# Input weights in quarters, GpSimd adding a token's two weighted expert rows, and later expert weight preparation, in a cross-attention and mixture-of-experts kernel

## The chip, the cores and the metric

The kernel runs on one core of one Trainium2 chip. The metric is device time in microseconds (us) of one execution. Before the change it is 1564.54 us, the median of 3 runs (1563.1 to 1567.49).

## What is computed

```python
x = x + xattn(layernorm(x), ctx_768, Wq, Wkv, Wproj, bproj)   # 16 heads of 64, softmax over 128 keys
x = x + ffn(layernorm(x), gate_w, expert_w, expert_b, combine_w)

# ffn, for each token:
probs = softmax(tokens @ gate_w.T)                 # 8 experts
w, idx = top_k(probs, 2)
expert_out = silu(tokens @ expert_w[e].T + expert_b[e])
mixed = w[0] * expert_out[idx[0]] + w[1] * expert_out[idx[1]]
out = mixed @ combine_w.T
```

There are 64 sequences of 128 tokens with 256 features, and a context of 128 rows of 192 features for each. All is float32. Products are made of three matrix products on operands split into a rounded high part and a rest (names ending in `_hi` and `_lo`).

## The kernel before, in words

Two sequences make a pair; there are 32 pairs, numbered i. A pair has 8 slots, one for each pair of heads, numbered u = 0 to 7; the slot number s is 8i + u. Every engine runs its own instruction stream over the same slots, in an order written out by hand, and semaphores tie the streams together. In slot s TensorE turns the probabilities of the slot before (`turn_probs`, tile pT_ps), makes queries and keys three slots ahead (`queries_keys`, qk_ps), scores one slot ahead (`scores`, s_ps), then "mid" jobs, then `attend` (o_ps) and `project` (proj_ps) for earlier slots, then "late" jobs. Slots -8 to -1 are the lead-in, and slots from 256 on are the tail.

Per slot ScalarE makes exponentials and high parts, VectorE row maxima, row sums and low parts. GpSimd normalises the probabilities (L1392), splits the attended rows (L1401 and L1403, `o_s_hi` and `o_s_lo`, which `project` waits for), issues indirect DMAs (scatters L1424, gathers L1437) and, where u = 0, adds the bias (L1410). Project for slot s needs the `o_s_lo` that GpSimd makes in the same slot.

The last four pairs (28 to 31) take all experts densely in the tail. The first 28 go through a sorted copy of their rows: blocks of 128 rows of one expert (`turn_block`, `expert`, in slots 78 to 259), and then a mix for each pair. For the mix of pair m GpSimd gathers four row sets of 128x256 into `got` (a part of `stage`), ScalarE multiplies them by their weights (`weigh`, L935) in a slot t of `plan.mix`, TensorE turns and adds them (`turn_mixed`, L681) in the mid of slot t + 1, VectorE makes the low part `mT_s_lo`, TensorE multiplies by the combine weights (`combine`) late in slot t + 2, and VectorE adds the residual (L1092) in slot t + 3. 23 mixes have t + 1 in a slot up to 256: eleven of them fall on u = 0 and eleven on u = 2 (in couples: 128 and 130, 136 and 138, 144 and 146, and so on), and one on slot 256. The gather of pair m waits until `turn_mixed` of pair m - 2 has read the same buffer.

The mid and late jobs share three PSUM banks, `gen_ps`, in turn: a job waits until the third job before it in the order has been drained.

The weights come in through `stage`. The first loads bring two of the eight head pairs' query and key columns (FIRST) and all values (VALUES); the other six follow as REST. ScalarE rounds them (L835), VectorE and GpSimd make the low parts: `weight_lo` on VectorE (L1012 for queries, L1016 for the rest) and on GpSimd (L1374). GpSimd has the REST keys and the projection (L1415, L1374). The `queries_keys` of head pair 2 waits for all of REST. Expert weights are loaded into `stage` from slot -1 on, prepared in slots 1 to 9 (VectorE L1027, ScalarE L835, GpSimd L1374) and stored to an expert table.

Of the kernel before, what the change touches and what calls it, by code (L numbers as in the profile page):

```python
# [5 lines left out]
P = 128  # L6
# [52 lines left out]
class Plan:  # L59


    def __init__(self, pairs):
# [42 lines left out]
        self.tail = [r for at, r in sorted(self.mix.items()) if at > SLOTS * pairs + 2]  # L105
        self.last = max(max(self.turn) + 4, max(self.mix) + 4)
        self.jobs_at, order = {}, []
        for s in range(-SLOTS, self.last + 1):
# [45 lines left out]
def xattn_moe_kernel(nc, x, ctxT, wq, wkv, wkv_rest, wproj, bproj, gateT, expertT, expert_b, combineT, out):  # L154
# [20 lines left out]
    with ExitStack() as stack:  # L175
# [55 lines left out]
        def carve(n, rows):  # L231
# [83 lines left out]
        w_in = [sem(f"w_in{n}") for n in range(12)]  # L315
# [39 lines left out]
        ctx_lo, probs_done, weighted = (  # L355
            sem(n) for n in ("ctx_lo", "probs_done", "weighted"))
# [17 lines left out]
        def blocks_in_ring(r, n):  # L374
# [4 lines left out]
        FIRST, REST, VALUES = slice(0, 2 * P), slice(2 * P, D), slice(D, 2 * D)  # L379
        raw_wq = stage[:, 0, :].rearrange("p (a n) -> p a n", a=2)  # L380
        in_wq = wq.rearrange("(a p) n -> p a n", p=P)
        WEIGHTS = [
            (in_wq[:, :, FIRST], raw_wq[:, :, FIRST]),
            (wkv[0:P, FIRST], stage[:, 1, FIRST]),
            (wkv_rest[:, FIRST], stage[:, 2, FIRST]),
            (wkv[0:P, VALUES], stage[:, 1, VALUES]),
            (wkv_rest[:, VALUES], stage[:, 2, VALUES]),
            (in_wq[:, :, REST], raw_wq[:, :, REST]),
            (wkv[0:P, REST], stage[:, 1, REST]),
            (wkv_rest[:, REST], stage[:, 2, REST]),  # L390
# [7 lines left out]
        SPLIT = [  # L398
            (raw_wq[:, :, FIRST], *[w[:, :, FIRST] for w in wq_s]),
            (stage[:, 1, FIRST], *[w[:, FIRST] for w in wkv0_s]),  # L400
            (stage[:, 2, FIRST], *[w[:, FIRST] for w in wkvr_s]),
            (stage[:, 1, VALUES], *[w[:, VALUES] for w in wkv0_s]),
            (stage[:, 2, VALUES], *[w[:, VALUES] for w in wkvr_s]),
            (raw_wq[:, :, REST], *[w[:, :, REST] for w in wq_s]),
            (stage[:, 1, REST], *[w[:, REST] for w in wkv0_s]),
            (stage[:, 2, REST], *[w[:, REST] for w in wkvr_s]),
            (stage[:, 3, :], *[w[:, :, :].rearrange("p g n -> p (g n)") for w in wproj_s]),
        ]
# [3 lines left out]

        FOR_FIRST, FOR_VALUES, BY_VECTOR, PROJECTION, EXPERTS_FROM, COMBINE_SPLIT = 3, 5, 6, 8, 9, len(SPLIT) - 1
        KEYS_BY_POOL = PROJECTION - BY_VECTOR
        PROJ_BY_POOL = KEYS_BY_POOL + 1
# [3 lines left out]
        def _(sp):  # L419
# [29 lines left out]
            def load_weights(n):  # L449

                if n >= EXPERTS_FROM:
                    sp.wait_ge(w_lo_dve, BY_VECTOR)
                if n > EXPERTS_FROM:
                    sp.wait_ge(w_lo_pool, KEYS_BY_POOL)
                of, to = WEIGHTS[n]
                sp.dma_start(to, of).then_inc(w_in[n], 16)
# [66 lines left out]
            for s, i, u in slots():  # L523
# [16 lines left out]
                if s == -1:  # L540
                    load_weights(EXPERTS_FROM)
                if s == 0:
# [6 lines left out]
                if s == 1:  # L549
                    load_weights(EXPERTS_FROM + 2)  # L550
                if 2 <= s < E - RING + 2:
                    load_last(s - 2 + RING)
                if 2 <= s < E + 2:
                    keep_expert(s - 2)
                if i == 1 and u == 0:
# [15 lines left out]
                if s - 3 in plan.mix:  # L571
                    r = plan.mix[s - 3]
# [3 lines left out]
                if s - 1 in plan.mix:  # L576
                    r = plan.mix[s - 1]
# [10 lines left out]
        def _(pe):  # L588
# [9 lines left out]
            def queries_keys(j, p):  # L598
# [4 lines left out]
                if j == 0 and p == 0:  # L603
                    pe.wait_ge(w_hi, FOR_FIRST)
                    pe.wait_ge(w_lo_dve, FOR_FIRST)
# [147 lines left out]
            def general(s, position):  # L753
                for kind, n in plan.jobs_at[s, position]:
# [32 lines left out]
            pe.wait_ge(const_b, 2)  # L787
            for s, i, u in slots():
# [29 lines left out]
        def _(act):  # L818
# [6 lines left out]
            def weight_hi(n):  # L825
# [9 lines left out]
                act.activation(hi, raw, ACT.Copy, scale=QSCALE if n in (0, FOR_VALUES) else 1.0).then_inc(w_hi, 1)  # L835
# [95 lines left out]
            def weigh(m):  # L931
                act.wait_ge(gathered[m % 2], 64 * (m // 2 + 1))
                act.wait_ge(top_w_done, m + 1)
                for k in range(4):
                    last = act.activation(got[m % 2][:, k, :], got[m % 2][:, k, :], ACT.Copy, scale=top_w[:, m, k:k + 1])  # L935
# [13 lines left out]
            for s, i, u in slots():  # L949
# [38 lines left out]
                if i == -1 and u == 5:  # L988
                    for n in range(FOR_VALUES, PROJECTION):
                        weight_hi(n)  # L990
                if 2 <= s < E + 2:
                    weight_hi(EXPERTS_FROM + s - 2)
# [3 lines left out]
                if i == 1 and u == 2:  # L996
# [4 lines left out]
        def _(dve):  # L1001
# [6 lines left out]
            def weight_lo(n):  # L1008
                dve.wait_ge(w_hi, n + 1)
                raw, hi, lo = SPLIT[n]  # L1010
                if n in (0, FOR_VALUES):
                    dve.scalar_tensor_tensor(out=lo, in0=raw, scalar=QSCALE, in1=hi.bitcast(F32),  # L1012
                                             op0=ALU.mult, op1=ALU.subtract).then_inc(w_lo_dve, 1)
                else:
                    rows = HALF if n in (2, 4) else P
# [518 lines left out]
```

## Time and profile before

| what | value |
|---|---|
| median of 3 runs | 1564.54 us |
| the profiled execution's own time | 1565.96 us |
| its span in the trace | 1564.2 us |
| TensorE matmul busy | 1499.4 us, 96% of the span |
| VectorE busy | 1279.3 us, 82% |
| ScalarE busy | 1071.5 us, 69% |
| GpSimd busy | 942.5 us, 60% |

PE is TensorE (PEld its weight loads), DVE VectorE, ACT ScalarE, POOL GpSimd, SP the engine that issues most DMAs. Times are from the start of the span. In rows, a bracket at the end gives the idle time of the engine before the instruction and what ended it. TensorE's rows overlap: an instruction's duration is longer than the step to the next, so steps between starts are what it costs on the path.

### The profile page before, as it was taken

To read this page: it belongs to the slowest core of one execution; us is meant where nothing else is said; L and a number is where in the kernel's file an instruction comes from. 1 tells how busy PE (TensorE), PEld (TensorE's weight loads), DVE (VectorE), ACT (ScalarE), POOL (GpSimd) and SP (SyncE) were. 2 spreads that over 40 slices of the span, in tenths; PEclk is the share of its full clock that TensorE was granted. 3 is DMA by queue.
4 is the path that set the end of the run, shared out by engine and by line. 5 is a ranking of instruction groups with operands and counts; after the bars stand their busy time and mean duration, and the time that the engine had idled before them with its cause. 6 is when DMAs were issued, how large, how long until landed. Compare 5 with 4: busy or idle time off the path is not lost.

```text
span 1564.2 us, 38447 instructions
## 1 busy us (share of the span) xinstructions
PE 1499.4 (96%) x11664; PEld 1435.4 (92%) x11664; DVE 1279.3 (82%) x3121; ACT 1071.5 (69%) x2923; POOL 942.5 (60%) x1239
## 2 busy tenths in 40 slices
PE   5999999999999999999999999999999999999878
PEld 5889999999899999999899999989999999999767
DVE  6978888888988888888988888888888888877556
ACT  4767666666677766777677676767776767667645
POOL 5756666666555555587666455576676556655624
PEclk9999999999999999999999999999999999999989
DMA  8543333333577777445688777658787777877913
GB/s 240 179 135 95 95 94 94 94 94 102 169 225 226 216 212 224 125 127 138 191 238 239 210 222 223 179 150 245 232 244 236 240 218 235 257 229 205 317 56 109
DMA packets 180475, 287.78 MB, mean 184 GB/s; under 512 B 23600, under 2 KB 115248, under 8 KB 180016
## 3 DMA queue, kind: packets, MB, share of 16 engines
q1 hardware_dynamic: 169520, 255.94, 57.1%
q0 software_dynamic: 10752, 29.37, 5.8%
q8 instruction: 97, 1.59, 0.5%
q14 instruction: 106, 0.87, 0.2%
HBM read 156.51 MB, written 61.60 MB: 139 GB/s over the span
## 4 chain that ended last, share of the span: by engine, by line
PE 72%; DVE 11%; issue 7%; ACT 5%; POOL 3%; DMA 1%; SPq 0%; ACTq 0%; DVEq 0%; POOLq 0%
PE gen_ps L591 19%; PE qk_ps L591 16%; PE o_ps L591 9%; PE proj_ps L591 9%; PE s_ps L591 8%; PE pT_ps L636 6%; PE gen_ps L714 2%; DVE neg_max L1063 1%; DVE sums L1070 1%; PE gen_ps L689 1%; PE gen_ps L681 1%; DVE pT_s_lo L1005 1%; ACT stage L822 1%; POOL stage L1437 1%; DMA k_s<-qk_s 1%
## 5 line engine op out<-in xcount | busy, mean ns | idle before, releaser
L1401 POOL CAST o_s_hi<-stage 128x256 fp32r<-128x256 f32 x256 | 102.0, 398 | 413.9 <-ACT stage L822 409.7
L848 ACT ACTIVATE stage<-s_ps,neg_max 128x128 f32<-128x128 f32 x1024 | 293.0, 372 | 72.9 <-DVE neg_max L1063 69.2
L1392 POOL TENSOR_TENSOR stage<-stage,inv_sums 128x512 f32<-128x512 f32 x256 | 266.2, 1040 | 10.8 <-DVE inv_sums L1072 10.7
L822 ACT CAST pT_s_hi<-pT_ps 128x512 fp32r<-128x512 f32 x256 | 150.7, 589 | 129.8 <-PE pT_ps L636 118.7
L591 PE MATMUL s_ps<-k_s,qk_s 128*128 128x256 f32 x1536 | 226.5, 283 | 3.1 <-DMA k_s<-qk_s 3.1
L1070 DVE TENSOR_REDUCE sums<-stage 128x4 f32<-128x512 f32 x256 | 172.8, 675 | 46.0 <-ACT stage L848 31.6
L1005 DVE TENSOR_TENSOR qk_s<-qk_ps,qk_s 128x512 fp32r<-128x512 f32 x256 | 176.4, 689 | 39.4 <-ACT qk_s L822 34.6
L591 PEld LDWEIGHTS s_ps<-k_s,qk_s 128*128 128x128 f32 x1536 | 201.6, 189 | 3.8 <-DMA k_s<-qk_s 3.5
L1403 POOL TENSOR_TENSOR o_s_lo<-stage,o_s_hi 128x256 fp32r<-128x256 f32 x256 | 188.4, 736 | 20.8
L1005 DVE TENSOR_TENSOR pT_s_lo<-pT_ps,pT_s_hi 128x512 fp32r<-128x512 f32 x256 | 171.9, 672 | 30.6 <-ACT pT_s_hi L822 24.5
L822 ACT CAST v_s_hi<-gen_ps 128x512 fp32r<-128x512 f32 x129 | 75.8, 588 | 176.6 <-PE gen_ps L591 172.5
L822 ACT COPY stage<-o_ps 64x256 f32<-64x256 f32 x512 | 188.0, 367 | 3.1
L591 PE MATMUL qk_ps<-xT_hi,wq_s_hi 128*128 128x256 f32 x512 | 166.0, 324 | 12.1 <-POOL wkvr_s_lo L1374 5.0
L1063 DVE TENSOR_REDUCE neg_max<-s_ps 128x4 f32<-128x512 f32 x256 | 174.5, 682 | 1.0 <-PE s_ps L591 1.0
L591 PE MATMUL o_ps<-pT_s_hi,v_s_hi 128*128 128x256 f32 x512 | 155.5, 304 | 16.2 <-DVE pT_s_lo L1005 14.3
L822 ACT CAST qk_s<-qk_ps 128x512 fp32r<-128x512 f32 x256 | 149.8, 585 | 29.9 <-PE qk_ps L591 20.6
L636 PE MATMUL pT_ps<-ident,stage 128*128 128x128 f32 x1024 | 154.8, 274 | 1.1 <-POOL stage L1392 0.7
L591 PE MATMUL proj_ps<-wproj_s_hi,o_s_hi 128*128 128x256 f32 x512 | 146.5, 286 | 3.3 <-POOL o_s_lo L1403 3.0
L591 PE MATMUL qk_ps<-xT_hi,wq_s_lo 128*128 128x256 f32 x512 | 145.0, 283 | 0.0
L591 PE MATMUL o_ps<-pT_s_hi,v_s_lo 128*128 128x256 f32 x512 | 144.9, 283 | 0.0
L591 PE MATMUL o_ps<-pT_s_lo,v_s_hi 128*128 128x256 f32 x512 | 144.5, 282 | 0.0
L591 PE MATMUL qk_ps<-xT_lo,wq_s_hi 128*128 128x256 f32 x512 | 144.2, 282 | 0.0
(367 smaller groups left out, 4681.4 us busy)
## 6 DMA issues: line engine op xcount, KB each, us to landing
w_block<-expert_table SPq DMA_DIRECT2D x147, 512.0 KB
k_s<-qk_s SPq DMA_DIRECT2D x512, 128.0 KB
stage<-sorted_x SPq DMA_DIRECT2D x147, 128.0 KB
sorted_y<-stage SPq DMA_DIRECT2D x147, 128.0 KB
x_raw<-in_x SPq DMA_DIRECT2D x32, 256.0 KB
c_raw<-in_ctxT SPq DMA_DIRECT2D x32, 256.0 KB
stage<-in_x SPq DMA_DIRECT2D x32, 256.0 KB
x_kept<-x SPq DMA_DIRECT2D x32, 256.0 KB
```

The costliest lines, as they stand in the source:

```text
L591: mm = pe.matmul(out_ap, l, r, start=start and n == 0, stop=stop and n == len(terms) - 1, skip_group_check=skip)
L636: mm = pe.transpose(pT_ps[:, k * P:(k + 1) * P], probs[p % 2][:, k, :], ident[:, :])
L681: mm = pe.matmul(bank[:, a * N2 + t * P:a * N2 + (t + 1) * P], rows(t, k)[:, a * P:(a + 1) * P], ident[:, :], is_transpose=True, start=k = ...
L714: mm = pe.transpose(bank[:, a * P:(a + 1) * P], x_block[n % RING][:, a * P:(a + 1) * P], ident[:, :])
L822: last = act.copy(to, of)
L848: last = act.activation(probs[p % 2][:, k, :], s_ps[:, k * P:(k + 1) * P], ACT.Exp, bias=neg_max[p % 2][:, k:k + 1])
L1005: last = dve.tensor_tensor(lo, of, hi.bitcast(F32), ALU.subtract)
L1063: dve.tensor_reduce(neg_max[p % 2][:, :], s_ps[:, :].rearrange("p (k n) -> p k n", k=4), AX_X, ALU.max, negate=True).then_inc(max_done, 1)
L1070: dve.tensor_reduce(sums[p % 2][:, :], probs[p % 2][:, :, :], AX_X, ALU.add).then_inc(sums_done, 1)
L1392: pool.tensor_tensor(probs[b][:, :, :], probs[b][:, :, :], inv_sums[b][:, :].unsqueeze(2).broadcast_to([P, 4, P]), ALU.mult).then_inc(prob ...
L1401: pool.tensor_copy(hi[:, :, :], o_full).then_inc(o_hi, 1)
L1403: pool.tensor_tensor(lo[:, :, :], o_full, hi[:, :, :].bitcast(F32), ALU.subtract).then_inc(o_lo, 1)
```

## The change

**Weights.** Query and key columns come in four parts of two head pairs each instead of one and a rest. ScalarE and VectorE split part 1 in slot -3, part 2 in slot -1 and part 3 in slot 1, GpSimd splits only the projection. Head pairs 2, 4 and 6 of pair 0 each wait for their own part. Expert weights are loaded from slot 2 instead of -1 and prepared in slots 5 to 13 instead of 1 to 9, the combine weights in slot 14 instead of 10, and the clearing of the dump rows is issued in slot 32 instead of 8. TensorE starts with 16 transposes of the identity into a bank that nobody reads.

**Mix.** `got` holds the first choices of both token groups and then the second choices. For the 23 mixes with t below 256, GpSimd adds the two halves in slot t + 1 (`add_rows`, one instruction of 128x512), TensorE turns the sum in slot t + 2 with 4 transposes instead of 8, and combine, residual, the load of the residual and the store move one slot later with it. The other 9 mixes keep their slots and their 8 transposes.

```diff
+        self.added_first = [r for at, r in sorted(self.mix.items()) if at < SLOTS * pairs]
+        self.mix_turn = {at + (2 if r in self.added_first else 1): r for at, r in self.mix.items()}
...
-            if s - 1 in self.mix:
-                mid.append(("turn_mixed", self.mix[s - 1]))
+            if s in self.mix_turn:
+                mid.append(("turn_mixed", self.mix_turn[s]))
...
-            if s - 2 in self.mix:
-                late.append(("combine", self.mix[s - 2]))
+            if s - 1 in self.mix_turn:
+                late.append(("combine", self.mix_turn[s - 1]))
...
+        PARTS = [slice(n * 2 * P, (n + 1) * 2 * P) for n in range(HEAD_PAIRS // 2)]
...
+        PART_AT = {-3: 1, -1: 2, 1: 3}
...
-                if j == 0 and p == 2:
-                    pe.wait_ge(w_hi, PROJECTION)
-                    pe.wait_ge(w_lo_dve, BY_VECTOR)
-                    pe.wait_ge(w_lo_pool, KEYS_BY_POOL)
+                if j == 0 and p % 2 == 0:
+                    pe.wait_ge(w_hi, keys_through(p // 2))
+                    pe.wait_ge(w_lo_dve, keys_through(p // 2))
...
-                        pe.wait_ge(weighted, m + 1)
-                        mm = turn_sum(lambda t, k: got[m % 2][:, 2 * t + k, :], bank)
+                        if n in plan.added_first:
+                            pe.wait_ge(rows_added, n + 1)
+                            mm = turn(got[m % 2][:, 0:2, :], bank)
+                        else:
+                            pe.wait_ge(weighted, m + 1)
+                            mm = turn_sum(lambda t, k: got[m % 2][:, t + 2 * k, :], bank)
...
+            for n in range(16):
+                pe.transpose(gen_ps[BANKS - 1][:, 0:P], ident[:, :], ident[:, :])
...
+            def add_rows(m):
+
+                pool.wait_ge(weighted, m + 1)
+                first, second = (got[m % 2][:, k:k + 2, :].rearrange("p t c -> p (t c)") for k in (0, 2))
+                pool.tensor_tensor(first, first, second, ALU.add).then_inc(rows_added, 1)
...
+                if plan.mix.get(s - 1) in plan.added_first:
+                    add_rows(plan.pair_of[plan.mix[s - 1]])
                 for m, k in plan.gather.get(s, []):
                     gather(m, k)
...
-                    for n in range(BY_VECTOR, PROJECTION):
-                        weight_lo(n)
                     split_projection()
```

On GpSimd, around the slots 136 to 138 (the mixes of pairs 2 and 3), the program before has these rows (names are tiles; `stage<-stage,inv_sums` is the normalised probabilities, `bias_row` the bias):

```order
L1401 CAST o_s_hi<-stage 128x256
L1403 TENSOR_TENSOR o_s_lo<-stage,o_s_hi 128x256
L1392 TENSOR_TENSOR stage<-stage,inv_sums 128x512
L1424 DMA sorted_x<-xn,row_of 80640x256
L1385 TENSOR_TENSOR var_eps<-mv,eps 128x2
L1387 TENSOR_TENSOR rstd<-var_eps,minus_half 128x2
```

and the changed one these, from the same cast of the slot with u = 2 on:

```order
L1411 CAST o_s_hi<-stage 128x256
L1413 TENSOR_TENSOR o_s_lo<-stage,o_s_hi 128x256
L1402 TENSOR_TENSOR stage<-stage,inv_sums 128x512
L1434 DMA sorted_x<-xn_0,row_of 80640x256
L1395 TENSOR_TENSOR var_eps<-mv,eps 128x2
L1397 TENSOR_TENSOR rstd<-var_eps,minus_half 128x2
L1463 TENSOR_TENSOR stage<-stage 128x512
```

The add of 128x512 is new behind the slot's other work; where u = 0 it stands between the scatter and the bias.

On VectorE, in the lead-in (slots -3 to 0 of the program), the rows before are:

```order
L1012 SCALAR_TENSOR_TENSOR wq_s_lo<-stage,wq_s_hi 128x2x768
L1005 TENSOR_TENSOR qk_s<-qk_ps,qk_s 128x2x256
L1005 TENSOR_TENSOR v_s_lo<-gen_ps,v_s_hi 128x512
L1005 TENSOR_TENSOR qk_s<-qk_ps,qk_s 128x2x256
L1063 TENSOR_REDUCE neg_max<-s_ps 128x4
L1070 TENSOR_REDUCE sums<-stage 128x4
```

and now, from the second quarter on (the first three rows are part 1, the last three before `sums` are part 2):

```order
L1021 SCALAR_TENSOR_TENSOR wq_s_lo<-stage,wq_s_hi 128x2x256
L1025 TENSOR_TENSOR wkv_s_lo<-stage,wkv_s_hi 128x256
L1025 TENSOR_TENSOR wkvr_s_lo<-stage,wkvr_s_hi 64x256
L1014 TENSOR_TENSOR qk_s<-qk_ps,qk_s 128x2x256
L1014 TENSOR_TENSOR v_s_lo<-gen_ps,v_s_hi 128x512
L1014 TENSOR_TENSOR qk_s<-qk_ps,qk_s 128x2x256
L1072 TENSOR_REDUCE neg_max<-s_ps 128x4
L1021 SCALAR_TENSOR_TENSOR wq_s_lo<-stage,wq_s_hi 128x2x256
L1025 TENSOR_TENSOR wkv_s_lo<-stage,wkv_s_hi 128x256
L1025 TENSOR_TENSOR wkvr_s_lo<-stage,wkvr_s_hi 64x256
L1079 TENSOR_REDUCE sums<-stage 128x4
```

Three splits of part 2 now stand between the first row maximum and the first row sums.

On TensorE, in slot 145 of the changed program, the mix's transposes stand behind the value job; before, 8 of them stood in slot 144 right behind the scores:

```order
L596 MATMUL gen_ps<-wkvr_s_hi,cT_hi 128x512
L596 MATMUL gen_ps<-wkvr_s_lo,cT_hi 128x512
L690 MATMUL gen_ps<-ident,stage 128x128 x4
L596 MATMUL o_ps<-pT_s_hi,v_s_hi 128x256
L596 MATMUL o_ps<-pT_s_lo,v_s_hi 128x256
```

So the four transposes come one slot later than the eight did, ahead of the same `attend`.

## Rows read from the trace of the kernel before

**Rows 1.** The page: busy time, share and instructions of each engine.

```profile
PE 1499.4 (96%) x11664; PEld 1435.4 (92%) x11664; DVE 1279.3 (82%) x3121; ACT 1071.5 (69%) x2923; POOL 942.5 (60%) x1239
```

**Rows 2.** Windows: slots 144 to 148 (two mixes), then 160 to 164 (none).

```profile
784.11:816.63 32.52, 32.37 (x265) 31.46 (x264) 27.71 (x58) 24.01 (x67) 20.20 (x26) 1.00 0.80 237
885.48:912.78 27.30, 27.30 (x225) 26.85 (x224) 23.85 (x53) 20.28 (x57) 17.82 (x23) 1.00 0.80 232
```

**Rows 3.** Timeline of slots 144 to 146: start, duration, engine, line.

```profile
786.79 1.04 PE L681 MATMUL gen_ps<-ident,stage 128*128 128x128 f32 x8
787.58 0.36 PE L591 MATMUL o_ps<-pT_s_hi,v_s_hi 128*128 128x256 f32 x1
788.38 0.28 PE L591 MATMUL proj_ps<-wproj_s_hi,o_s_hi 128*128 128x256 f32 x1
794.38 0.28 PE L591 MATMUL proj_ps<-wproj_s_hi,o_s_hi 128*128 128x256 f32 x1
799.18 0.88 PE L591 MATMUL s_ps<-k_s,qk_s 128*128 128x256 f32 x6
800.21 0.50 PE L591 MATMUL gen_ps<-wkv_s_hi,cT_hi 128*128 128x512 f32 x1
...
787.45 0.74 POOL L1403 TENSOR_TENSOR o_s_lo<-stage,o_s_hi 128x256 fp32r<-128x256 f32 x1
790.42 1.31 POOL L1410 TENSOR_TENSOR stage<-stage,bias_row 128x512 f32<-128x512 f32 x1
792.27 0.74 POOL L1403 TENSOR_TENSOR o_s_lo<-stage,o_s_hi 128x256 fp32r<-128x256 f32 x1
```

**Rows 4.** VectorE beside GpSimd: slots 144 and 136, and a wait of TensorE.

```profile
790.16 1.61 DVE L1147 SCALAR_TENSOR_TENSOR top_w<-gate_exp,gate_inv 128x4 f32<-128x4 f32 x1
742.88 1.98 DVE L1218 TENSOR_SCALAR rounded<-rounded 128x9 f32<-128x9 f32 x1
748.07 0.38 PE L591 MATMUL o_ps<-pT_s_hi,v_s_hi 128*128 128x256 f32 x1 [1.90 <-DVE pT_s_lo L1005]
```

**Rows 5.** Timeline of the lead-in, GpSimd and TensorE.

```profile
19.01 2.65 POOL L1374 TENSOR_TENSOR wkv_s_lo<-stage,wkv_s_hi 128x768 fp32r<-128x768 f32 x1 [11.36 <-ACT wkv_s_hi L835]
21.62 1.80 POOL L1374 TENSOR_TENSOR wkvr_s_lo<-stage,wkvr_s_hi 128x768 fp32r<-128x768 f32 x1
25.33 4.56 POOL L1374 TENSOR_TENSOR wproj_s_lo<-stage,wproj_s_hi 128x2048 fp32r<-128x2048 f32 x1
11.36 0.55 PE L591 MATMUL qk_ps<-xT_hi,wq_s_hi 128*128 128x256 f32 x1 [2.01 <-DVE xT_lo L1005]
15.98 0.36 PE L591 MATMUL qk_ps<-xT_hi,wq_s_hi 128*128 128x256 f32 x1
23.67 0.55 PE L591 MATMUL qk_ps<-xT_hi,wq_s_hi 128*128 128x256 f32 x1 [5.00 <-POOL wkvr_s_lo L1374]
31.66 0.66 PE L636 MATMUL pT_ps<-ident,stage 128*128 128x128 f32 x4 [0.69 <-POOL stage L1392]
```

**Rows 6.** DMA issues of the first 60 us: KB and us to landing.

```profile
stage<-in_wproj SPq DMA_DIRECT2D x1, 1024.0 KB, 12.0
```

**Rows 7.** Windows: the wait of 5 us, and what follows (granted clock third from the end).

```profile
23.60:29.80 6.20, 6.00 (x26) 5.74 (x27) 1.57 (x3) 1.73 (x5) 6.12 (x2) 0.50 0.50 181
29.80:36.20 6.40, 5.71 (x42) 5.14 (x41) 5.54 (x14) 3.16 (x8) 2.80 (x5) 1.00 1.01 233
```

**Rows 8.** Timeline: a wait in slot 10, then the tail.

```profile
82.14 0.97 PE L591 MATMUL s_ps<-k_s,qk_s 128*128 128x256 f32 x6 [2.41 <-DMA k_s<-qk_s]
...
1464.71 0.98 POOL L1437 DMA_INDIRECT stage<-sorted_y,y_row_of  x1 [0.16 <-DMA sorted_y<-stage]
1470.40 0.38 PE L591 MATMUL proj_ps<-wproj_s_hi,o_s_hi 128*128 128x256 f32 x1 [1.10 <-POOL o_s_lo L1403]
1478.84 1.09 PE L681 MATMUL gen_ps<-ident,stage 128*128 128x128 f32 x8 [2.31 <-DVE stage L1086]
1490.58 0.69 DVE L1165 SCALAR_TENSOR_TENSOR x_raw<-stage,pT_ps 128x512 f32<-128x512 f32 x1 [4.61 <-POOL last_row L1447]
```

More of the change, by code:

```diff
@@ L314, in xattn_moe_kernel @@
             sem(n) for n in ("x_in", "c_in", "xres_in", "gate_in", "bias_in", "biased"))
-        w_in = [sem(f"w_in{n}") for n in range(12)]
+        w_in = [sem(f"w_in{n}") for n in range(18)]
         table_stored = [sem(f"table_stored{r}") for r in range(RING)]
@@ L354, in xattn_moe_kernel @@
         ctx_rest = sem("ctx_rest")
[L355 to L356 removed]
+        ctx_lo, probs_done, weighted, rows_added = (
+            sem(n) for n in ("ctx_lo", "probs_done", "weighted", "rows_added"))
         eps_done = [sem(f"eps_done{n}") for n in (1, 2)]
@@ L396, in xattn_moe_kernel @@
         ]
[L398 to L408, printed above, removed]
+        SPLIT.append((stage[:, 3, :], *[w[:, :, :].rearrange("p g n -> p (g n)") for w in wproj_s]))
         for e in range(E):
@@ L548, in _ @@
                         load_last(e)
-                if s == 1:
+                if s == 4:
                     load_weights(EXPERTS_FROM + 2)
[L551 to L555, printed above, removed]
+                if EXPERTS_AT <= s < EXPERTS_AT + E - RING:
+                    load_last(s - EXPERTS_AT + RING)
+                if EXPERTS_AT <= s < EXPERTS_AT + E:
+                    keep_expert(s - EXPERTS_AT)
+                if i == 4 and u == 0:
                     sp.wait_ge(zero_ready, 1)
@@ L570, in _ @@
                     load_experts(1)
-                if s - 3 in plan.mix:
-                    r = plan.mix[s - 3]
+                if s - 2 in plan.mix_turn:
+                    r = plan.mix_turn[s - 2]
                     sp.wait_ge(drained["combine"], r + 1)
@@ L575, in _ @@
                         out_stored[r % 3], 16)
-                if s - 1 in plan.mix:
-                    r = plan.mix[s - 1]
+                if s in plan.mix_turn:
+                    r = plan.mix_turn[s]
                     m = plan.pair_of[r]
@@ L934, in weigh @@
                 for k in range(4):
-                    last = act.activation(got[m % 2][:, k, :], got[m % 2][:, k, :], ACT.Copy, scale=top_w[:, m, k:k + 1])
+                    rows = got[m % 2][:, k // 2 + 2 * (k % 2), :]
+                    last = act.activation(rows, rows, ACT.Copy, scale=top_w[:, m, k:k + 1])
                 last.then_inc(weighted, 1)
@@ L987, in _ @@
                         weight_hi(n)
-                if i == -1 and u == 5:
-                    for n in range(FOR_VALUES, PROJECTION):
+                if s in PART_AT:
+                    for n in keys_of(PART_AT[s]):
                         weight_hi(n)
-                if 2 <= s < E + 2:
-                    weight_hi(EXPERTS_FROM + s - 2)
+                if EXPERTS_AT <= s < EXPERTS_AT + E:
+                    weight_hi(EXPERTS_FROM + s - EXPERTS_AT)
                 if i == 0 and u == 1:
@@ L995, in _ @@
                     act.copy(wgate[:, :, 0:E], gate_raw[:, :, :]).then_inc(gate_w_ready, 1)
-                if i == 1 and u == 2:
+                if s == EXPERTS_AT + E:
                     weight_hi(COMBINE_SPLIT)
@@ L1014, in weight_lo @@
                 else:
-                    rows = HALF if n in (2, 4) else P
+                    rows = HALF if n in HALF_ROWS else P
                     dve.tensor_tensor(lo[0:rows, :], raw[0:rows, :], hi[0:rows, :].bitcast(F32),
@@ L1300, in _ @@
                     expert_out(plan.turn[s - 2][2])
-                if s - 3 in plan.mix:
-                    combined(plan.mix[s - 3])
+                if s - 2 in plan.mix_turn:
+                    combined(plan.mix_turn[s - 2])
                 if u < 5 and now:
@@ L1350, in _ @@
                         weight_lo(n)
-                if i == -1 and u == 5:
-                    weight_lo(FOR_VALUES)
+                if s in PART_AT:
+                    for n in keys_of(PART_AT[s]):
+                        weight_lo(n)
                 if i == 0 and u == 0:
```

60 lines of the change are left out of this document (31 added, 29 removed).

## The prediction

> **What bounds the kernel now.** I read the page first: TensorE's matmuls fill 96% of the span, the next engine 82% [rows 1]. Then windows over the same five slots with and without two mixes. With them 32.52 us, of which TensorE is busy 32.37; without them 27.30 of 27.30 [rows 2]. So in the steady part a mix costs (32.52 - 27.30) / 2 = 2.6 us, nearly all of it TensorE's own work, and a microsecond taken from TensorE's stream counts only where no other engine's result is waited for next. That made me read the timeline of one couple of mixes (slots 144 and 146) row by row [rows 3], then the places where VectorE and GpSimd hold each other up [rows 4], then the lead-in with its DMA and its clock [rows 5 to 7], and last the tail [rows 8]. The profiled execution took 1565.96 us, 1.4 above the median of the runs; I sum against it and take 1.4 off.
>
> **Mix: what leaves TensorE.** The 8 transposes start at 786.79 and the next `attend` at 787.58 [rows 3]: 0.79 us, 0.10 each, with 0.08 of pipeline in a gap behind them 0.87. Four fewer give 4 x 0.11 = 0.43. Over 23 mixes that is 10 us, the ceiling. What of it arrives depends on what TensorE would then wait for. I follow the couple 144 to 149:
>
> - Slot 144 loses all 8. But `project` at 788.38 needs `o_s_lo`, which ends at 787.45 + 0.74 = 788.19 [rows 3]. TensorE gets 0.19 earlier there, not 0.87. In the other couples I read 0.1 to 0.8, about 0.35 on average: -0.35.
> - Slot 146 loses all 8 too: -0.87. Slots 145 and 147 gain 4 each: +0.43 and +0.43.
> - The three `gen_ps` banks: behind the last score of slot 146 (six that start at 799.18 and, with 0.88 for all six step by (0.88 - 0.28) / 5 = 0.12, so the value job could follow at about 799.9) the value job starts only at 800.21 [rows 3]. That wait of 0.31 for a bank goes (-0.31), and a smaller one of the same kind in slot 148, which I put at half of it (-0.15). With the job order moved one slot on, waits of these two sizes should come back in slots 147 (about 0.4, since the value job there meets a bank drained later) and 149 (about 0.16).
>
> Sum: -0.35 - 0.87 - 0.31 - 0.15 + 0.43 + 0.43 + 0.41 + 0.16 = -0.25 for a couple. Its ends: -0.87 (2 x 0.43 arrives whole), and +0.2 if the old waits stay beside the new ones. Eight couples by -0.25: -2.
>
> **Mix: what is added to GpSimd.** `add_rows` is 128x512, two operands in SBUF. The trace has no such add; the nearest row is the bias, 128x512, 1.31 us [rows 3], so I take 1.3. Lower end 1.3; upper end by the row of another two-operand GpSimd instruction beside VectorE: 128x768 took 2.65 us [rows 5] where the next of the same form took 1.80, so +0.85, 2.15. For mixes whose turn was on u = 0 the add stands in slot 144 before the bias; queued behind it are the bias and slot 145's `o_s_hi` and `o_s_lo`. The `o_s_lo` of 145 ends at 792.27 + 0.74 = 793.01, and `project` wants it at 794.38 [rows 3]: slack 1.37. An add of 1.3 fits in, just. For u = 2 it is the last of its slot and hides wholly; what it costs if that cover goes is what the next `o_s_lo` is late, again 1:1.
>
> GpSimd's adds also hold up VectorE. In slot 144 a VectorE instruction on 128x4 took 1.61 us while GpSimd added the bias from 790.42 to 791.73 [rows 3, 4]: it ended with that add. In slot 136 one on 128x9 took 1.98 us likewise, and TensorE then waited 1.90 us for `pT_s_lo` [rows 4]. This belongs to slots where VectorE ends a chain of block counts. There are such places in three couples (136, 216, 232), and in them the order changes: the add is ahead of the bias and the transposes behind it in time, so part of a wait of 1.3 to 1.9 is filled with the moved 4 transposes and another part moves off. I take -0.9 for each, -2.7; ends 0 and -1.9 each.
>
> The Trainium skill says the same of the port (page "GPSIMD Engine Reference", section 8, key points): GpSimd shares its SBUF interface with VectorE, and contention comes with VectorE instructions in a two-port mode or with two SBUF inputs. By that rule the new add would be stretched wherever VectorE runs such an instruction, and would stretch those in turn; [rows 4] agree for VectorE's side. A mechanism of this kernel by which it decides is rival C below.
>
> Together the mixing gives -2 - 2.7 = -4.7; I take -4.5 since one more mix, the one of slot 256, is in the tail's sum. Ends: -10, the ceiling, and +1.6 (8 x 0.2). Combine, residual, load and store only move by a slot; they carry the same rows, and VectorE's and the queues' load in a slot of 144 to 149 leaves room.
>
> **Weights: the start.** Today TensorE waits 5.00 us up to 23.67 for GpSimd's split of the REST keys and values, and then the first `turn_probs` at 31.66 waits for GpSimd again [rows 5]. GpSimd's order is REST splits (one 2.65, a second 1.80, ending 23.42), the projection's cast (begun then, before 25.33) and its split of 4.56 (ending 25.33 + 4.56 = 29.89), and only then the probabilities, which `turn_probs` waits for. After the change GpSimd has only the projection. It can begin when `in_wproj` has landed, today 12.0 us after issue [rows 6], at 19.8; behind six more issues of smaller transfers I take 21. Then 21 + 1.9 + 4.6 = 27.5 (cast 25.33 - 23.42 = 1.9, split 4.6). So the 5.00 us wait ends about 4 us earlier (part 1 by 19.6).
>
> But this isn't what sets slot 0. On VectorE part 2 now stands between the first row maximum and the first `sums`; three splits which I put at 1.5 us together (half the columns of GpSimd's 128x768 row of 1.80 and less for each [rows 5]) and which cannot run beside GpSimd's 4.56 (as in [rows 4]) and so end near 28.5. From the end of GpSimd's split to `turn_probs` it is 31.66 - 29.89 = 1.8 today, and now 0.5 more for the sums behind the splits: `turn_probs` at about 30.8 instead of 31.66 (27.4 to 31.5 as the landing and the blocking go). TensorE stands idle before that for some 5 us instead of 5 us earlier.
>
> Behind a 5.00 us wait today the granted clock is 0.50 for the next 6.2 us, then 1.00 [rows 7]; that is the lower of the levels 1.2 and 2.4 GHz. With the idle stretch ahead of slot 0 the same may follow there, where TensorE's work is dense: 26 matmuls in 6.20 us now, 42 in the 6.40 us behind [rows 7], so a slow stretch costs 2 to 3 us. Against -0.9 that makes +1 to +2. The Trainium skill (page "TensorE: Matmul & The Clock Gate", Part 1) has the engine throttled by default and released by activity; the rows agree, and the sum stays by the rows.
>
> The 16 opening transposes are meant for the first matmuls: from 11.36 to 15.98 they go at 0.21 a step, then 0.12 [rows 5], so up to 2 us. These end in a wait for weights anyway: 0.
>
> Expert preparation moves by about four slots: slots 2 to 4 lose some splitting on each of three engines and slots 10 to 13 gain it; these engines have room in both (82% and less [rows 1]). The wait of 2.41 us in slot 10 for `k_s` [rows 8] comes with the burst of dump row clears and table stores; it goes, and partly returns at slot 32, -1. Start and early slots together: 0; ends -4 (first probabilities at 27.4, clock kept, wait of slot 10 gone) and +3.
>
> **Tail.** GpSimd's gather for the third last sorted mix is issued at 1464.71 [rows 8]. It waits for the `turn_mixed` two mixes earlier, which now stands in slot 257, between its scores and the `project` of 1470.40, about 1469.2. Queued behind the gather is slot 256's `o_s_lo`, for which `project` already waits 1.10 us up to 1470.40 [rows 8]: by the issue's delay of 4.5 less 0.6 of slack there, that goes to about 1474.3, +3.9. TensorE then gets back a combine (12 matmuls at 0.12, 1.4) that left this slot and the 2.31 of idle time before the transposes at 1478.84 [rows 8]. On GpSimd's own chain, which ends in the 4.61 wait at 1490.58 [rows 8], about 0.9 is left. I take +1, ends -1 and +3.
>
> Sum: -4.5 + 0 + 1 = -3.5; 1565.96 - 3.5 = 1562.5, less 1.4: **1561.0 us**.
>
> **The rivals.** 0.3% is 4.7 us, about what these runs can tell from no change.
>
> - **A, the sum above**, 1561.0, own range 1558 to 1564. Chance 0.45.
> - **B, nearly all of TensorE's saving arrives**: 23 x 0.43 = 10, since 96% busy says that slack is rare [rows 1], and `project` is only held in slot 144's way where `o_s_lo` is that close. Against: it is that close there. 1554.5. Chance 0.27.
> - **C, slower**: the add is stretched by VectorE's accesses. It decides from 1.37 us on; at 2.15 each of 11 couples makes TensorE wait 0.85 more for `project` in the slot after, +9.4, so 1561 + 9.4 = 1570.4. For: 2.65 against 1.80 [rows 5]. Against: the bias at 790.42 kept 1.31 while VectorE had one pending [rows 3, 4], so it is VectorE that waited there. Chance 0.13.
> - **D, nothing to be measured**: the adds and moved waits take what the transposes give, or a slow start of 3 us does. 1564.5. Chance 0.15.
>
> **How the numbers follow.** The range 1554.5 to 1567.5 holds A and D and the half of B above its centre (0.74), and the milder part of C (an add of up to 1.9): about 0.8. Faster: B whole and the lower 0.13 of A (below 1559.8), 0.40. Slower: C with 0.01 of D, 0.14. Same: the rest, 0.46.
>
> **What would show it.** Four `turn_mixed` transposes per mix at about 0.43 us. In slot 144 `project` about 0.2 earlier than now with its wait named `o_s_lo`; if 0.8 earlier, B. `add_rows` at 1.3 us; at 2 or more, with `project` of slot 145 waiting for `o_s_lo`, C. VectorE's 128x4 instruction again ending with a GpSimd add. At the start: `queries` of head pair 2 near 19.6, first `turn_probs` near 30.8, and a granted clock of 0.50 behind it. In the tail the project of 1470.40 about 4 us later against its slot. The prediction would be wrong most easily by slot 0 coming much earlier than 30.8 or by the bank waits of slots 147 and 149 being absent.

## The result, and the profile after

The changed kernel takes 1573.11 us, the median of 6 runs (1568.46 to 1574.45), against 1566.01 for 6 runs of the kernel before. The ratio is 1.0044, with a 95% interval of 1.0028 to 1.006: slower by some 7 us, where 3.5 us faster was forecast. The profiled execution took 1574.45 us. One of the six executions of the kernel e4 below took 1649.82 us at a lower clock; it counts in that kernel's median and not in its ratio.

The page of the changed kernel, busy time of each engine and the granted clock in 40 slices, then the groups of GpSimd's adds and of the transposes that turn their sums (busy, mean ns):

```profile
span 1572.4 us, 38334 instructions
PE 1504.5 (96%) x11588; PEld 1436.6 (91%) x11588; DVE 1280.4 (81%) x3129; ACT 1070.3 (68%) x2929; POOL 967.5 (62%) x1260
...
PEclk8999999999999999999999999999999999999979
```

```profile
L1463 POOL TENSOR_TENSOR stage<-stage 128x512 f32<-128x512 f32 x23 | 29.7, 1291 | 0.3
L690 PE MATMUL gen_ps<-ident,stage 128*128 128x128 f32 x92 | 15.4, 293 | 5.9 <-DVE stage L1095 5.9
```

TensorE has fewer matmuls and is busy 5.1 us longer than in [rows 1]: 92 transposes stand for 184, and yet work got slower somewhere. The add takes 1.29 us, as forecast (1.3). The clock shows a dip in the last but one slice.

Where the time went is best seen by the start of each slot (the first transpose of `turn_probs`), after minus before, in us: -1.9 at slot 20, -1.1 at 128, -0.7 at 136, -4.9 at 216, -3.2 at 222, -1.2 at 238, -1.4 at 255. So up to the tail the changed kernel is still ahead. Then the windows of the two tails, from the start of slot 255 to the last matmul, before and after:

```profile
1456.58:1559.93 103.35, 85.69 (x490) 72.83 (x488) 59.18 (x127) 55.35 (x127) 44.09 (x54) 0.95 0.45 148
```

```profile
1455.23:1569.03 113.80, 89.37 (x486) 76.34 (x484) 60.30 (x127) 55.48 (x127) 45.32 (x55) 0.90 0.39 130
```

The tail is 10.4 us longer (113.80 - 103.35), and its mean clock 0.90 instead of 0.95 (third number from the end). In this pair of profiles the whole loss lies here: -1.4 + 10.4 = 9.0, against 8.2 between the two spans; behind the last matmul the changed kernel needs 0.9 us less (1572.4 - 1569.03 against 1564.2 - 1559.93).

### The profile page after: what moved, and what is told of

The parts are those of the page before. It is cut to its first block, busy times and chain, and to the rows that moved or that the text cites. A ratio compares the mean times of both kernels' runs of the same rounds, so it can differ in the third digit from the quotient of the medians.

```text
span 1572.4 us, 38334 instructions
## 1 busy us (share of the span) xinstructions
PE 1504.5 (96%) x11588; PEld 1436.6 (91%) x11588; DVE 1280.4 (81%) x3129; ACT 1070.3 (68%) x2929; POOL 967.5 (62%) x1260
## 4 chain that ended last, share of the span: by engine, by line
PE 74%; DVE 12%; issue 6%; ACT 4%; POOL 2%; SPq 1%; DMA 0%; ACTq 0%; DVEq 0%; POOLq 0%
PE gen_ps L596 20%; PE qk_ps L596 17%; PE o_ps L596 10%; PE proj_ps L596 9%; PE s_ps L596 9%; PE pT_ps L637 6%; PE gen_ps L690 2%; PE gen_ps L715 2%; DVE sums L1079 2%; DVE neg_max L1072 1%; DVE pT_s_lo L1014 1%; POOL stage L1447 1%; DVE xn L1059 1%; ACT stage L830 1%; ACT qk_s L830 1%
## 5 line engine op out<-in xcount | busy, mean ns | idle before, releaser
L596 PE MATMUL proj_ps<-wproj_s_hi,o_s_lo 128*128 128x256 f32 x512 | 144.7, 283 | 0.0
```

What stands on the lines that cost most here:

```text
L596: mm = pe.matmul(out_ap, l, r, start=start and n == 0, stop=stop and n == len(terms) - 1, skip_group_check=skip)
```

## The tail

The changed kernel's timeline in slot 256, GpSimd and TensorE:

```profile
1463.14 1.28 POOL L1463 TENSOR_TENSOR stage<-stage 128x512 f32<-128x512 f32 x1
1469.18 1.03 POOL L1447 DMA_INDIRECT stage<-sorted_y,y_row_of  x1 [4.75 <-PE gen_ps L690]
1471.51 0.95 POOL L1447 DMA_INDIRECT stage<-sorted_y,y_row_of  x1 [1.30 <-issue]
1472.47 1.28 POOL L1420 TENSOR_TENSOR stage<-stage,bias_row 128x512 f32<-128x512 f32 x1
1473.67 0.41 POOL L1411 CAST o_s_hi<-stage 128x256 fp32r<-128x256 f32 x1
1474.16 0.72 POOL L1413 TENSOR_TENSOR o_s_lo<-stage,o_s_hi 128x256 fp32r<-128x256 f32 x1
...
1474.94 0.58 PE L596 MATMUL proj_ps<-wproj_s_hi,o_s_hi 128*128 128x256 f32 x1 [6.55 <-POOL o_s_lo L1413]
```

The gather waits 4.75 us for the late `turn_mixed`, and behind it on GpSimd's queue stand a second gather, the bias, and the `o_s_lo` for which `project` waits 6.55 us, where it waited 1.10 [rows 8]. The windows of that wait and of what follows:

```profile
1468.40:1474.94 6.54, 0.00 (x0) 0.00 (x1) 2.47 (x6) 3.11 (x8) 4.32 (x5) 0.90 0.87 322
1474.94:1481.50 6.56, 6.56 (x23) 5.78 (x24) 1.09 (x2) 0.98 (x2) 1.93 (x2) 0.58 0.39 106
```

TensorE is idle for 6.5 us and then, at a granted clock of 0.58, mostly at the lower of its two levels, does 23 matmuls in 6.56 us. The prediction had this path, with its wait 3.9 us later, but it let 2.3 us of idle time and a moved combine take 2.9 of it back, and had no slow stretch behind the wait.

The delay and the slow stretch can be told apart. The kernel e4 below has the same tail, and its profile the same wait of `project`. TensorE there, the windows of the wait and of what follows, and the whole tail from slot 255 on:

```profile
1483.60 0.58 PE L593 MATMUL proj_ps<-wproj_s_hi,o_s_hi 128*128 128x256 f32 x1 [6.54 <-POOL o_s_lo L1410]
...
1477.06:1483.60 6.54, 0.00 (x1) 0.00 (x0) 2.47 (x6) 3.12 (x8) 4.32 (x5) 0.72 0.64 234
1483.60:1490.16 6.56, 6.56 (x32) 5.91 (x33) 1.38 (x2) 1.61 (x4) 1.93 (x2) 0.76 0.37 107
1463.89:1572.97 109.08, 84.64 (x486) 72.24 (x484) 60.30 (x127) 55.38 (x127) 45.34 (x55) 0.94 0.39 128
```

The clock had fallen already within the wait (0.72) and was 0.76 behind it, and the tail took 109.08 us, 5.7 more than before. So of the 10.4 us some 5.8 are the late `project`, and 4.7 (113.80 - 109.08) come with the lower clock of the one execution: 0.58 instead of 0.76 behind the wait, and 0.90 instead of 0.94 over the tail.

## The chain of block counts

VectorE, GpSimd and TensorE of the changed kernel in slots 216 and 217, where the prediction took off 0.9 us:

```profile
1215.00 3.23 DVE L1227 TENSOR_SCALAR rounded<-rounded 128x9 f32<-128x9 f32 x1
...
1215.63 1.31 POOL L1463 TENSOR_TENSOR stage<-stage 128x512 f32<-128x512 f32 x1
1216.89 1.30 POOL L1420 TENSOR_TENSOR stage<-stage,bias_row 128x512 f32<-128x512 f32 x1
...
1221.75 0.48 PE L690 MATMUL gen_ps<-ident,stage 128*128 128x128 f32 x1 [2.79 <-DVE stage L1095]
```

An instruction on 128x9, which takes 0.18 us alone, takes 3.23: it ends only when both GpSimd instructions of 128x512, which run back to back, have ended (1216.89 + 1.30 = 1218.19); the cast of `o_s_hi` that GpSimd begins next (1218.12) no longer holds it. Before, its like took 1.79, and slot 217 was 8.96 us long with 1.30 of waiting in it; now, in the windows' row:

```profile
1214.98:1225.63 10.65, 7.86 (x53) 7.30 (x51) 10.32 (x21) 6.12 (x17) 6.36 (x7) 0.84 0.76 235
1218.00:1221.70 3.70, 0.96 (x5) 0.45 (x3) 3.46 (x12) 0.64 (x2) 2.10 (x4) 0.92 0.55 192
1221.70:1225.63 3.93, 3.88 (x23) 3.88 (x23) 3.86 (x10) 2.67 (x8) 1.26 (x2) 0.64 0.88 271
```

Here too the clock falls behind the wait, to 0.64. Slot 233 is 10.90 us long against 8.91 in the same way. But the fall is not part of every execution. In the kernel e1 below, which has the same code here, slot 233 has a wait of 2.77 us and keeps its clock:

```profile
1317.76:1327.15 9.39, 6.62 (x53) 6.06 (x51) 9.12 (x17) 5.33 (x15) 6.44 (x7) 1.00 0.71 217
```

It is 9.39 us long. So of the 2.0 us that slot 233 is longer, 0.5 is the longer wait, less the transposes that left, and 1.5 the clock.

## The experiments

All counts are of mixes that GpSimd adds. The set is one line of the planner, `added_first`; each kernel but e4 is the changed kernel with this edit. Where the set no longer begins with the first mix or has gaps (e2, e5, e7 to e11), the count that TensorE waits for is the place in the set instead of the mix's number. `before` is run beside each; its medians were 1567.24, 1567.75 and 1567.5 us in the three groups (e1 to e4, e5 to e8, e9 to e11). The ratios are estimated from the runs and are not the quotients of the medians; they lie up to 0.0013 apart (e7: 0.9939 by the medians), and where they differ the ratio with its interval counts.

| kernel | adds | median, us | ratio to before | 95% interval |
|---|---|---|---|---|
| changed | 23 | 1573.11 | 1.0044 | 1.0028 to 1.006 |
| e1 without the tail's mix | 22 | 1570.54 | 1.0025 | 1.0015 to 1.0035 |
| e2 and without three at chain ends | 19 | 1563.41 | 0.9976 | 0.9964 to 0.9989 |
| e3 weights alone | 0 | 1564.28 | 0.9984 | 0.9971 to 0.9997 |
| e4 mix alone | 23 | 1580.13 | 1.009 | 1.0072 to 1.0107 |
| e5 as e2, without slot 250 | 18 | 1561.94 | 0.9972 | 0.9959 to 0.9984 |
| e6 22 moved, none added | 0 | 1570.12 | 1.0017 | 1.0004 to 1.003 |
| e7 only u = 2 | 10 | 1558.16 | 0.9952 | 0.9935 to 0.9969 |
| e8 only the tail's mix | 1 | 1574.15 | 1.0048 | 1.003 to 1.0067 |
| e9 as e8, two gathers later | 1 | 1566.32 | 0.9991 | 0.9978 to 1.0004 |
| e10 as e7, no opening transposes | 10 | 1561.00 | 0.9963 | 0.995 to 0.9977 |
| e11 e7 again | 10 | 1559.90 | 0.9956 | 0.994 to 0.9971 |

**e1.**

```diff
-... if at < SLOTS * pairs]
+... if at < SLOTS * pairs - 1]
```

> The changed kernel, but the mix whose turn stood in slot 256 keeps its old slot and its 8 transposes; 22 mixes are still added by GpSimd. My theory (the moved turn of that mix holds up GpSimd's next gather, the o_s_lo queued behind it, and then a project for 6.55 us, after which the granted clock is 0.58): the 10.4 us that the tail lost from slot 255 on come back nearly whole, the wait of project falls to about 1.1 us, and the kernel is 1 to 3 us faster than before. Rival (the add and the moved jobs cost TensorE time everywhere): still at least 5 us slower than before.

The tail came back whole: `project` waits 1.07 us, and from the start of slot 255 it is 102.8 us to the start of the last matmul, where before has 103.1 and the changed kernel 113.5. But the kernel stayed slower than before by 0.25%. My sum of the rest was wrong: in this execution slot 255 begins 4.3 us later than before, not 1.4 earlier. The same code up to slot 255 had slots of other lengths: slot 186, right behind a wait of 1.73 us in slot 185, took 6.59 us here at a clock of 0.74, and 5.05 in the changed kernel's profile at 1.00. Windows of e1, slots 185 and 186, and of the changed kernel:

```profile
1022.09:1029.19 7.10, 5.37 (x38) 4.80 (x39) 6.82 (x14) 3.49 (x11) 5.41 (x6) 1.00 0.35 96
1029.19:1035.78 6.59, 6.59 (x41) 6.37 (x40) 5.53 (x15) 3.76 (x12) 3.29 (x5) 0.74 0.44 119
```

```profile
1021.71:1028.82 7.11, 5.37 (x38) 4.80 (x39) 6.82 (x14) 3.49 (x11) 5.41 (x6) 1.00 0.35 96
1028.82:1033.87 5.05, 5.05 (x40) 4.83 (x39) 4.88 (x15) 3.09 (x9) 2.98 (x5) 1.00 0.45 130
```

So a wait of 1.7 us is sometimes followed by a slow stretch that costs 1.5 us, and sometimes not. All 13 kernels have this wait in slot 185 (1.72 to 1.76 us): in ten profiles slot 186 took 5.04 to 5.06 us, in three (e1, e7 and e9) 6.56 to 6.60. Single executions of a kernel lie up to 6 us beside its median (in e8 1568.38 against 1574.15), and so the table decides, not one profile. By its ratios the tail's mix costs only 0.2% on top of the other 22 (e1 against the changed kernel), and 0.64% with none (e8 against e3). Why these differ is left open; that the clock's part of the tail's loss comes and goes, as in e4, may belong to it.

**e2.**

```diff
+... if at < SLOTS * pairs - 1 and at not in (135, 215, 231)]
```

> As the kernel above, and the three mixes whose turn stood in slots 136, 216 and 232, where VectorE ends a chain of block counts, keep their slots and 8 transposes too. Theory (there the add and the bias run back to back on GpSimd and hold one small VectorE instruction for 3.23 us): slots 217 and 233 return from 10.65 and 10.90 us to about 8.9, their VectorE instruction to about 1.8, and the kernel is 4 to 7 us faster than before, 3 to 5 faster than the one above. Rival (the later slot of the mix does it, not the add): the long VectorE instruction and the wait stay, gain under 1 us.

7 us faster than e1, more than expected; 3.8 faster than before, a little under what was expected. Slot 217 took 8.92 us and the first row of its block count 1.81. The profiles of e1 and e2 give 3.1 us over slots 216 to 221, 1.5 over 232 to 237 and 0.7 over 136 to 141, 5.3 of the 7. So the three mixes on u = 0 at chain ends were a loss of the mix part, not a gain; those on u = 2 of the same couples are still added here, and slots 216 to 221 are 1.1 us shorter than before.

**e3.**

```diff
+... if at < 0]
```

> The weights part and all else of the change, but no mix is added by GpSimd: all 32 keep their slots and 8 transposes. Theory (weights in parts gain 1.9 us up to slot 20, which stays): 1 to 3 us faster than before. Rival (the lower clock behind the start costs more than it gains, or the later expert preparation costs at slot 73): no gain or slower by more than 1 us.

As expected, 3 us by the medians. The theory holds: in its profile it is 4.3 us ahead of before at slot 8 and 6.7 at slot 11, since the wait of 2.41 us in slot 10 [rows 8] is gone. Slots 11, 12 and 15 then take 3.1 us more, with waits of 0.6 to 1.0 us. They do so in every kernel with the weights part, and not in e4, so this is the later expert preparation, and 3.5 us are left at slot 16. The rival falls.

**e4.** The other way round: the kernel before with the mix part only (`added_first`, `mix_turn`, `add_rows`, `turn`, the order of `got`, as in the diff of the change).

> The kernel before with the mix part alone, 23 mixes added by GpSimd; the weights stay as before. Theory (the parts add up, and the mix part holds the whole loss): 7 to 10 us slower than before. Rival (the parts disturb each other, for example since the whole program runs shifted): under 5 us slower.

12.9 us slower, more than the 7 to 10 expected: the weights part's 3.0 and the changed kernel's 7.1 would add to 10.1. By the ratios it is 1.0044 / 0.9984 = 1.006 against 1.009, and their intervals only just meet, so that the two parts simply add up is not shown. The mix part holds the whole loss.

**e5.**

```diff
+... if at < SLOTS * pairs - 1 and at not in (135, 215, 231, 249)]
```

> As the kernel that left out the tail's mix and the three at chain ends, and the mix whose turn stood in slot 250 keeps its old slots too; 18 mixes are added by GpSimd. Theory (with its combine in slot 252 the gate matmuls of slot 253 wait 1.3 to 1.5 us for a bank that VectorE has not drained, and the clock may fall after it): slot 253 returns from 7.5 to 4.8 us, and the kernel is 5 to 8 us faster than before (1563.41 for the one above, now about 2.5 less). Rival (the wait of slot 253 is older than the mix change): no gain over the one above.

No difference shown in the whole (0.9972 against 0.9976), clear in the slots: slot 253, which in e2 took 7.54 us, is back at 4.77. But slots 250 and 251 took 2.5 us more than in e3, since the combine of the mix ahead now stands in slot 250 beside this mix's 8 transposes, and slot 251 has a wait of 0.96 us. The rival, that the wait of slot 253 is older than the mix change, falls. TensorE in slot 253 of e2:

```profile
1444.21 0.28 PE L596 MATMUL gen_ps<-wgate,xT_hi 128*128 128x16 f32 x1 [1.50 <-DVE stage L1095]
```

The gate's first matmul waits for a bank of `gen_ps` that VectorE has not yet drained. In before, slot 253 had 0.11 us of idle time and was 4.78 long.

**e6.** With the line of e1, and:

```diff
-                            pe.wait_ge(rows_added, n + 1)
-                            mm = turn(got[m % 2][:, 0:2, :], bank)
+                            pe.wait_ge(weighted, m + 1)
+                            mm = turn_sum(lambda t, k: got[m % 2][:, t + 2 * k, :], bank)
...
-                if plan.mix.get(s - 1) in plan.added_first:
-                    add_rows(plan.pair_of[plan.mix[s - 1]])
```

> The 22 mixes move one slot later as in the kernel that left out the tail's mix alone, but GpSimd adds nothing and TensorE turns all with 8 transposes: the slots are moved, the add isn't there. Theory (the add holds VectorE at the chain ends): the small VectorE instruction of slots 217 and 233 takes 1.8 us or less instead of 3.23 and TensorE waits 1.3 there instead of 2.8; the wait of slot 253 stays, since it comes from the move. About 0 to 3 us slower than the weights part alone (1564.28), thus within 2 us of before. Rival (the move itself costs at the chain ends): 217 and 233 stay at 10 us or more, and the kernel is over 5 us slower than before.

At the chain end the theory is right. VectorE in slot 217 of e6:

```profile
1220.40 1.98 DVE L1227 TENSOR_SCALAR rounded<-rounded 128x9 f32<-128x9 f32 x1
```

1.98 us with one GpSimd instruction, 3.22 in e1 with two in a row; TensorE waits 1.60 there instead of 2.78, and the slot takes 8.69 us instead of 10.35. In the whole it is 2.4 us slower than before by the medians, and 5.8 than e3 (5.2 by the ratios): more than I had put down. Moving a couple costs by itself. Against e3, slots 152 to 157 changed by -0.26, -0.56, +0.15, -0.16, +1.19 and +0.13, together +0.49; with the adds (e5) by -0.27, -0.98, +0.17, -0.58, +1.19 and +0.12, together -0.35. So in this couple the adds bring the full 0.42 each, and the move takes 0.49. Over the seven couples outside the chain ends and slots 248 to 253 (those at 128, 144, 152, 192, 200, 208 and 240), e6 is 0.4 to 0.8 us longer than before in each.

**e7.**

```diff
+... if at < SLOTS * pairs - 1 and at % SLOTS == 1 and at != 249]
```

> Only the ten mixes whose turn stood on u = 2 (without the one of slot 250) are added by GpSimd. Theory (there the add is hidden behind no other GpSimd work in the way, and TensorE gets four transposes less): 10 x 0.43 = 4 us faster than the weights part alone, so 6 to 8 faster than before. Rival (a bank wait of 0.4 us one slot later takes each gain back): like the weights part alone, 2 to 4 us faster than before.

The fastest kernel, 0.48% faster than before: against e3 5 us by the ratios, where 4 was expected. Against e3 the slots 152 to 157 changed by +0.03, +0.01, -0.84, -1.01, +1.16 and +0.12, together -0.53: one added mix brings more than the two of e5 with their -0.35. So here the mix on u = 0 loses 0.18 us, although its four transposes less are 0.42. Over the seven couples e5 is up to 0.9 us longer than e7, 0.3 on average.

**e8.**

```diff
+... if at == SLOTS * pairs - 1]
```

> The only mix added by GpSimd is the one whose turn stood in slot 256; all others keep their slots and 8 transposes. Theory (this one mix costs the tail 10 us by the gather that waits for its turn): 6 to 9 us slower than before, 9 to 11 slower than the weights part alone, with a project that waits over 6 us in slot 256. Rival (the tail's loss needs the other mixes too, since the program arrives there otherwise): under 3 us slower than before.

9.9 us slower than e3, as expected, with a `project` that waits 6.54 us. One mix of 23 carries that loss without the others. TensorE there, and the window behind the wait:

```profile
1474.46 0.58 PE L596 MATMUL proj_ps<-wproj_s_hi,o_s_hi 128*128 128x256 f32 x1 [6.54 <-POOL o_s_lo L1413]
```

```profile
1474.00:1481.00 7.00, 6.54 (x23) 5.76 (x24) 1.08 (x2) 0.98 (x2) 2.33 (x3) 0.57 0.39 126
```

**e9.** As e8, and the gathers of slot 256 stand one slot later, behind that slot's bias and the next `o_s_lo`:

```diff
+        self.gather[SLOTS * pairs + 1] = self.gather.pop(SLOTS * pairs) + self.gather[SLOTS * pairs + 1]
```

> As the kernel in which only the tail's mix is added (1574.15, 1.0048 of before), but GpSimd issues the two gathers of slot 256 one slot later, behind the bias and the o_s_lo that project waits for; the mix's own add, turn and combine stay one slot later. Theory (what costs 10 us is the place of these gathers on GpSimd's queue, between the late turn and o_s_lo): project waits under 1.5 us there, and at least 7 of the 10 us come back, so 0 to 3 us faster than before. Rival (the late turn, combine or the add itself costs it): at least 5 us slower than before, as without this edit.

7.8 us come back by the medians, 8.9 by the ratios (0.9991 against 1.0048). The late turn, its combine and the add are all still there, so the place of the gathers does nearly all of it. About 1 us against e3 is left by the ratios, and 2.1 in the profiles from slot 255 on (104.20 against 102.08). GpSimd of e9, and the window in which the one above was slow:

```profile
1470.98 0.73 POOL L1415 TENSOR_TENSOR o_s_lo<-stage,o_s_hi 128x256 fp32r<-128x256 f32 x1
1474.04 1.04 POOL L1449 DMA_INDIRECT stage<-sorted_y,y_row_of  x1 [2.33 <-PE gen_ps L692]
```

```profile
1474.00:1481.00 7.00, 4.88 (x28) 4.04 (x28) 4.71 (x11) 4.50 (x11) 3.86 (x4) 1.00 1.05 387
```

The gather still waits, 2.33 us, but with the `o_s_lo` out of its way, and the clock stays at 1.00. The project has no wait left to be named.

**e10 and e11.**

```diff
-            for n in range(16):
-                pe.transpose(gen_ps[BANKS - 1][:, 0:P], ident[:, :], ident[:, :])
```

> As the kernel in which only the ten mixes on u = 2 are added (1558.16), but without TensorE's 16 opening transposes. Theory (they only speed matmuls that end in a wait for weights): within 1 us of the same kernel with them. Rival (a good part of the 2 us gained up to slot 1 comes from them): 1.5 us or more slower than with them.

> The kernel in which only the ten mixes on u = 2 are added, once more, on the same chip as the two above, as the base for the one without opening transposes. If 1558.16 stands for it, 7 to 10 us faster than before; if that was a lucky chip, 5 or less.

Within 1 us was expected of e10 if these transposes gain nothing. It is 1.1 us between them, and their intervals overlap for the most part: no difference is shown, and a gain of 1 us by the opening transposes isn't excluded. e7 stands: 0.9956 the second time.

## Right and wrong, step by step

**The tail, forecast +1, measured +10.4: the step that failed most.** It said that `project` would come about 3.9 us later and that a combine and "the 2.31 of idle time" would give 2.9 of it back. `project` came 5.9 us later against slot 255's start (19.71 against 13.82): the delayed gather was followed on GpSimd by a second one 2.33 us later, the bias and the splits. And nothing was given back: even in e4's profile, with a clock of 0.76 behind the wait, the tail is longer by the whole delay, 5.7 us, and in this one, at 0.58, by 10.4. e8 and e9 show that it is this mix, and the place of the gathers.

**The chain ends, forecast -2.7 together, measured a loss.** The step saw that a GpSimd instruction holds a VectorE one for its whole length, and took it that the added instruction would fill an existing wait. It put the add directly ahead of the bias, and the two hold VectorE together, 3.23 us. In the changed kernel's profile slots 136 to 141 took 0.4 us more than before, 216 to 221 1.6 more and 232 to 237 2.1 more, +4.1 together, part of it the lower clock behind the waits (slot 233 in e1). Slots 136 to 141 can't settle it: in e3, which adds no mix, they too were 1.3 us longer than before, with a clock of 0.83 in slot 137 where before had 1.00. The Trainium skill (page "GPSIMD Engine Reference", section 8) warns of the shared interface, and this trace agrees and gives the price. Rival C had the right resource and the wrong victim: the add was never stretched (1.29 us in 23); VectorE's instruction was.

**The couples, forecast -0.25 each, measured -0.1 on average in e1, e2, e4 and e5, and -0.6 in the changed kernel's own profile (the seven couples, against before).** Single ones lie between +0.4 (128 to 133) and -1.2 (144 to 149) in that profile; why it differs from e1's, with the same code, is open. The terms of the sum were right in kind: four transposes less bring 0.42 each, and moving a couple costs, but 0.6 on average (e6) and so more than the sum had. Two details were not right. In this profile `project` of slot 144 came 0.87 earlier, for `o_s_lo` came earlier too; in e1, e2 and e4 slot 144 had 0.4 to 0.5 of idle time and was as long as before. And both mixes were treated alike, where e7 shows that u = 2 brings all the gain (-0.4 a couple against before) and u = 0 takes 0.3 of it back.

**Slot 253, not in the sum.** The moved combine of the mix on slot 250 makes a wait of 1.3 to 1.5 us for a bank, +1.2 to +2.9 in five profiles (the lower ones at a clock of 1.00, the others at 0.78 to 0.81). The prediction counted bank waits in one couple and took them for all eight; this couple, in slots that have no value jobs, is another.

**The start, forecast 0, measured -1.9 in this profile and -3.0 by medians (e3).** The mechanism at the first `turn_probs` came as told: it starts at 29.99 (forecast 30.8, in the range), behind a wait and with a slow clock after it. The lead-in of the changed kernel, GpSimd, VectorE, TensorE, and the window behind:

```profile
22.21 4.58 POOL L1384 TENSOR_TENSOR wproj_s_lo<-stage,wproj_s_hi 128x2048 fp32r<-128x2048 f32 x1
...
24.52 2.81 DVE L1021 SCALAR_TENSOR_TENSOR wq_s_lo<-stage,wq_s_hi 128x512 fp32r<-128x512 f32 x1
...
29.99 1.12 PE L637 MATMUL pT_ps<-ident,stage 128*128 128x128 f32 x4 [3.11 <-POOL stage L1402]
```

```profile
29.99:35.86 5.87, 5.87 (x32) 5.63 (x33) 3.69 (x10) 2.82 (x8) 1.90 (x3) 0.72 0.21 47
```

VectorE's split was held until GpSimd's 4.58 us had ended, as forecast. The slow stretch is no fixed price either: the slot that it opens (slot 1 of the program, the prediction's slot 0) was 4.60 us long before, and 5.87 here at a clock of 0.72, but 4.40 in e3 and e11 at 1.00, and 7.03 to 7.06 in e5 and e7. Where the sum went wrong is the moved preparation, which it named and priced at nothing: slots 3, 4 and 5 lost 2.3 us, where waits of 0.35 to 1.05 us went, and slots 11, 12 and 15 took 3.1 more. The wait of slot 10, priced at -1, brought -2.3, for nothing of it came back at slot 32. That these nearly cancel, so that the total lay inside its range, is luck as much as sense. In e9 and e10 slot 5 had a wait of 2.2 to 2.5 us for the load of `k_s` and took 3 us more than before.

**The sum.** The changed kernel's profile against the one of before: -1.9 up to slot 20; +0.8 from there to 128, slots 73 to 75 +1.1, where the clock fell behind a wait that before has too (1.74 us), and the rest -0.3; the three couples at chain ends +4.1; slot 253 +1.2; the other couples and the slots beside them -5.5; the tail +10.4; behind the last matmul -0.9. Together 8.2, the difference of the spans. Of the forecast's three terms, mixing (-4.5) came out at -0.2 with slot 253, start and early slots (0) at -1.1, and the tail (+1) at +10.4, less the 0.9. Slower had a chance of 0.14, nearly all of it on another mechanism.

## What to carry to other kernels

Where a job is moved one slot later, follow who waits for it through every in-order queue: here a gather on GpSimd waited for a late transpose, with a split behind it for which TensorE stood still, and one mix of 23 cost 10 us. Two GpSimd adds of 128x512 in a row held a VectorE instruction for both, so place an added one apart from the next. Price an idle stretch of TensorE with the slow stretch that may follow it, compare more than one profile, and add only those jobs that pay: here the ten on u = 2.

## What the hardware showed

What the clock does behind a short wait differs from one execution to the next. Behind 1.73 us of waiting in slot 185 the granted clock was 1.00 in ten profiles and 0.74 or 0.75 in three, 1.5 us apart. Behind 6.5 us it was 0.57 and 0.58 in two of the three profiles in which that wait stood; in the third it fell within the wait and was 0.76 behind it. Behind 2.79 us it was 0.64 (slot 217), and behind 2.77 us 1.00 (slot 233 of e1). The Trainium skill (page "TensorE: Matmul & The Clock Gate", Part 1) says that the engine is throttled by default and released by activity; these rows agree in kind.
